# Returned rows two partitions apart, one halved expert fewer, and reordered transfers in a kernel of three expert layers and a convolution

## The chip, the cores and the metric

The kernel runs on one core of one Trainium2 chip. The metric is device time in microseconds (us), lower is better. A core has TensorE (PE in the profile, with PEld for its weight loads), VectorE (DVE), ScalarE (ACT), GpSimd (POOL) and SyncE (SP), which here issues all the DMA transfers.

## The reference

x is (2, 8, 256, 256): two batches b, eight channels or experts e, 256 tokens n, 256 features d. All is float32. Four blocks follow each other, each behind a group norm over pairs of channels:

```python
def _gn(v, G=4, eps=1e-05):
    g = v.reshape(B_, G, C_ // G, H_, W_)
    m, s = mean and var of g over (2, 3, 4)
    return ((g - m) / sqrt(s + eps)).reshape(v.shape)

x = x + L0(_gn(x))      # per expert e: gelu(x[b,e] @ w1[e] + b1[e]) @ w2[e] + b2[e], hidden width 1024
x = x + L1(_gn(x))      # 3x3 convolution over (n, d), 8 to 8 channels, edges repeated,
                        # weights sign(w) * mean(|w|), plus a bias per output channel
x = x + L2(_gn(x))      # like L0
x = x + L3(_gn(x))      # like L0, with the exact gelu
```

So a channel pair must be complete, in both tokens and features, before the group norm of the next block can be applied to it.

## The kernel before

**Data.** Features lie on the partitions: XT holds feature d = 128 c + p at partition p, chunk c. Twenty-four experts E0 to E23 are worked one after the other, eight per layer. An expert has eight units t, one per 128 hidden columns. A unit is six matmuls of the first product (`g1`, line 1016, into a G1 bank) and six of the second (`g2`, lines 1034 to 1039, into an ACC bank). Both products split each operand in a high part (float32r) and the rest: Xh and Xl, W1h and W1l, W2h and W2l, Hh and Hl. ACT makes the high parts and the gelu, DVE the rests by subtraction. TensorE runs `g2` two units behind `g1`. A normal expert has both batches side by side, 512 columns. A halved expert runs its eight units for one batch and then for the other, 256 columns each. Halved are E7, E8 and E9; E8 and E9 are also crossed (E8 batch 0, E9 batch 0, E8 batch 1, E9 batch 1).

**Weights.** SP loads each expert's W1 and W2 (1 MB each) into one W1raw and one W2raw. A load waits until the expert before has been split. ACT (`w_hi`) and DVE (`w_lo`) split an expert's eight pieces k = 0 to 7 in the eight units of the expert before.

**Statistics.** A job J sums a channel pair (`sums`, bn_stats, line 653), aggregates, and TensorE averages mean and variance over the partitions (lines 995 and 1001). POOL raises to the power -0.5 (line 493), DVE writes scale and shift (`scale_shift`), normalises (`norm`, line 709), and `x_hi` and `x_lo` (lines 553 and 714) split the result.

**Convolution.** The results of layer 0 are stored to DRAM by `store_x1` and loaded by `load_xc` into XC, whose partition is 8 j + channel: 16 rows of d (14 results) for 8 channels in one block, 19 blocks per batch, the last one shifted to fit. Two blocks are a tile; there are 20 tiles q, ten per batch, the tenth of a batch with one block. For a tile POOL makes CN (line 499, waits for the rest `Cl` of two tiles before), ACT the high part Ch (617), DVE the rest Cl (894), TensorE six matmuls with BAND (1122), ACT scales in PSUM (622), DVE adds to XC (903). Four PSUM banks rotate, CN has two buffers, Ch and Cl three; Ch and Cl lie on the memory of Hh and Hl.

**The way home.** For each block SP issues `give_back` (line 436): 14 rows of 8 channels, 112 partitions of XC, to 14 adjoining partitions of XT, 8 KB in each. A block that crosses d = 128 takes two. That is 40 transfers. E9's weights are loaded ahead of them. DVE sums batch 0 of channels 0 and 1 (job 9) at tile 17 and waits there for all of batch 0's transfers (`x2_in[0]`); the sums of batch 1 (job 10) are in E9's first unit. SP's queue is in order: the store and load of channel 7 for batch 1, then the `give_back` of tiles 0 to 19, then the next weights.

**The start.** TensorE transposes the first x tiles (982), runs filler matmuls (`stay_busy`, 989, two matmuls per count), and E0 begins when Xh, Xl and the four pieces of W1 are split. E1's pieces are split in the units 0 to 7 of E0. Pairs of experts in the middle of a layer are run in loops with register addresses.

Of the kernel before, what the change touches and what calls it, by code (L numbers as in the profile page):

```python
# [72 lines left out]
def units(E):

    return 2 * HT if isinstance(E, int) and E in HALVED else HT

def order(P):

    if isinstance(P, int) and 2 * P in CROSSED:
        return [(ee, b * HT + t) for b in range(B) for ee in range(2) for t in range(HT)]
    return [(ee, t) for ee in range(2) for t in range(units(2 * P + ee if isinstance(P, int) else None))]

def slots(E, layer=None):

    return HT * (E + sum(E > h for h in HALVED)) if isinstance(E, int) else (  # L90
        HT * E + (len(HALVED) * HT if layer else 0))

def slot_of(E, t, layer=None):

    if isinstance(E, int) and E in CROSSED:
        return slots(C) + (t // HT * 2 + E - C) * HT + t % HT
    return slots(E, layer) + t

def norm_of(E, b):

    return 2 * C + 2 * b + E - C if isinstance(E, int) and E in CROSSED else 2 * E + b

def evicts(E, layer=None):

    return DC * (E + sum(E > h for h in HALVED)) if isinstance(E, int) else (
        DC * E + (len(HALVED) * DC if layer else 0))

def evicts_for(E, b, layer):

    if not isinstance(E, int):
        return evicts(E - 1, layer)
    if E == C - 1:
        return evicts(E) if b else evicts(E - 1)
    if E in CROSSED:
        return evicts(C) + (2 * b + E - C - 1) * DC if b or E > C else evicts(C)  # L120
    return evicts(E) - DC if E == C + 2 else evicts(E - 1)

ONE_BATCH = {7: 0, 8: 1, 9: 0, 10: 1}

def batches(J):

    return (ONE_BATCH[J],) if isinstance(J, int) and J in ONE_BATCH else tuple(range(B))

def jobs_weighed(J, late):

    return B * J - sum(J > j for j in ONE_BATCH) if isinstance(J, int) else B * J - (len(ONE_BATCH) if late else 0)

USUAL = dict(sums=0, aggregate=1, mean=3, deviate=3, variance=5, eps=6, scale=7)

def jobs_of(P, ee, f):

    if not isinstance(P, int):
        if f == 0:
            return [(2 * P + ee, USUAL, 2 * P - 2 if ee else 2 * P + 2, P - 1 if ee else NPAIR)]  # L150
        return [] if ee else [(P + 7, USUAL, 2 * (P - NPAIR * f) + 2, NPAIR)]
    E = 2 * P + ee
    if E == 0:
        return [(1, dict(sums=4, aggregate=5, mean=7, deviate=7), 2, NPAIR)]
    if E == 1:
        return [(1, dict(variance=0, eps=0, scale=1), 2, NPAIR)]
    if E == 7:
        return [(6, dict(sums=0, aggregate=1, mean=4, deviate=4, variance=6, eps=7, scale=8), 4, 2),
                (7, dict(sums=10, aggregate=11, mean=12, deviate=12, variance=13, eps=13, scale=14), 6, 3)]
    if E == C:  # L160
        return [(11, dict(mean=9, deviate=9, variance=11, eps=11, scale=12), 2, NPAIR)]
    if E == C + 1:
        return [(10, dict(sums=0, aggregate=0, mean=2, deviate=2, variance=3, eps=4, scale=4), 0, NPAIR),
                (11, dict(sums=5, more_sums=6, aggregate=7), 2, NPAIR)]
    if P >= 5 and ee == 0 and P + 1 < LAYERS * NPAIR:
        return [(P + 7, USUAL, (2 * P + 2) % C, NPAIR)]
    return []

def job_for(P, f):  # L170

    if isinstance(P, int):
        return {0: 0, 1: 1, 2: 2, 3: 4, 4: 10}.get(P, P + 6)
    return P if f == 0 else P + 6

def known(value):

    return value if isinstance(value, int) else -1

def norms_of(P, ee, f):

    E = 2 * P + ee
    if isinstance(P, int) and E in HALVED:
        return {C - 1: {}, C: {5: (C + 1, 0, 9), 10: (C + 1, 1, 10), 13: (C + 2, 0, 11)},
                C + 1: {5: (C, 1, 10), 9: (C + 2, 1, 11)}}[E]
    if isinstance(P, int) and E == LAYERS * C - 1:
        return {}
    if ee and f == 0 and not isinstance(P, int):  # L190
        J = 2 * P
    else:
        J = job_for(P + 1 if ee else P, f)
    return {2: (E + 1, 0, J), 4: (E + 1, 1, J)}
# [968 lines left out]
```

## Time and profile before

| | |
|---|---|
| median of 3 runs | 615.67 us (614.67 to 615.85) |
| the profiled execution's own time | 614.43 us |
| its span, first to last instruction | 612.4 us |
| PE busy | 594.5 us (97%) |
| DVE busy | 423.2 us (69%) |
| ACT busy | 430.3 us (70%) |
| POOL busy | 31.3 us (5%) |
| mean granted TensorE clock | 0.989 of full |

Times in the trace are counted from the first instruction. The end of a matmul is modelled, so the distance between two starts says more than one duration. "Idle before" names what ended the wait.

### The profile page before, as it was taken

Reading aid. Unit: us, or ns where it says so; the run is one execution under the profiler, and the core shown is the slowest. Engines: PE = TensorE matmul, PEld = TensorE weight load, DVE = VectorE, ACT = ScalarE, POOL = GpSimd, SP = SyncE. Lnnn points to the kernel's source line nnn. Section 1 sums busy time; section 2 is a strip of 40 time slices with the busy share of each in tenths; the row PEclk is TensorE's granted clock in tenths of the full one; section 3 lists DMA queues with packets and bytes.
Section 4 is the critical chain, followed back from the end, with each engine's and each line's share of the span. In section 5 each row is a group of like instructions: output and inputs, shape, how many; then the busy total and the mean of one; then the engine's idle time right before and its main releaser. Section 6 shows DMA issues by size and latency. Waiting matters only on the chain.

```text
span 612.4 us, 9520 instructions
## 1 busy us (share of the span) xinstructions
PE 594.5 (97%) x2973; PEld 501.0 (82%) x2973; DVE 423.2 (69%) x857; ACT 430.3 (70%) x741; POOL 31.3 (5%) x52
## 2 busy tenths in 40 slices
PE   7999999999999896999999999999999999999997
PEld 7778888888889775999888888888888888888885
DVE  4867968768787796767865866866775675675532
ACT  5766767677777685769867777777767777777743
POOL 2000000000000451000000000000000000000000
PEclk9999999999999997999999999999999999999999
DMA  8673355455363599801332323223234244234001
GB/s 273 188 238 105 113 163 176 119 165 152 108 178 103 197 116 110 177 2 63 109 105 77 130 68 118 88 74 133 70 109 132 86 123 136 86 116 142 17 19 69
DMA packets 56342, 72.80 MB, mean 119 GB/s; under 512 B 4064, under 2 KB 50160, under 8 KB 56304
## 3 DMA queue, kind: packets, MB, share of 16 engines
q1 hardware_dynamic: 56304, 72.33, 41.5%
q8 instruction: 19, 0.31, 0.2%
q14 instruction: 19, 0.16, 0.1%
HBM read 59.70 MB, written 8.42 MB: 111 GB/s over the span
## 4 chain that ended last, share of the span: by engine, by line
PE 87%; DVE 4%; DMA 2%; issue 2%; SPq 2%; POOL 1%; ACT 1%; DVEq 0%; POOLq 0%; ACTq 0%
PE G L1016 42%; PE ACC L1039 14%; PE ACC L1034 14%; PE ACC L1035 14%; DMA W2raw<-in_L_conv_w 1%; DVE Cl L894 1%; DMA XT<-XC 1%; PE TR L1052 1%; SPq L374 1%; DVE XC L903 1%; DVE BN L653 1%; SPq L436 1%; PE ACC L1122 1%; PE TR L982 1%; PE STAT L995 0%
## 5 line engine op out<-in xcount | busy, mean ns | idle before, releaser
L720 DVE TENSOR_TENSOR Hl<-HR,Hh 128x512 fp32r<-128x512 f32 (+1 forms) x216 | 136.2, 631 | 158.8 <-ACT Hh L563 157.5
L559 ACT ACTIVATE HR<-G,BT 128x512 f32<-128x512 f32 (+1 forms) x216 | 138.3, 640 | 137.1 <-PE G L1016 135.9
L1016 PE MATMUL G<-Xh,W1l 128*128 128x512 f32 (+1 forms) x432 | 163.9, 379 | 3.3 <-issue 1.9
L1016 PE MATMUL G<-Xl,W1h 128*128 128x512 f32 (+1 forms) x432 | 158.7, 367 | 0.0
L1016 PE MATMUL G<-Xh,W1h 128*128 128x512 f32 (+1 forms) x432 | 158.5, 367 | 0.0
L1034 PE MATMUL ACC<-Hh,W2l 128*128 128x512 f32 (+1 forms) x432 | 156.5, 367 | 0.0
L1035 PE MATMUL ACC<-Hh,W2h 128*128 128x512 f32 (+1 forms) x432 | 156.2, 366 | 0.0
L563 ACT ACTIVATE Hh<-HR 128x512 fp32r<-128x512 f32 (+1 forms) x216 | 126.3, 585 | 8.7
L1039 PE MATMUL ACC<-Hl,W2h 128*128 128x512 f32 (+1 forms) x432 | 123.5, 367 | 0.6 <-DVE Hl L720 0.6
L1016 PEld LDWEIGHTS G<-Xh,W1l 128*128 128x128 f32 x432 | 82.0, 190 | 16.1 <-issue 2.2
L1016 PEld LDWEIGHTS G<-Xh,W1h 128*128 128x128 f32 x432 | 81.9, 189 | 13.6
L1034 PEld LDWEIGHTS ACC<-Hh,W2l 128*128 128x128 f32 x432 | 81.8, 189 | 13.4
L1035 PEld LDWEIGHTS ACC<-Hh,W2h 128*128 128x128 f32 x432 | 81.8, 189 | 13.2
L1016 PEld LDWEIGHTS G<-Xl,W1h 128*128 128x128 f32 x432 | 82.1, 190 | 11.5
L1039 PEld LDWEIGHTS ACC<-Hl,W2h 128*128 128x128 f32 x432 | 78.2, 189 | 14.5 <-DVE Hl L720 1.3
L699 DVE TENSOR_TENSOR W2l<-W2raw,W2h 128x512 fp32r<-128x512 f32 x96 | 65.6, 686 | 4.2 <-ACT W2h L546 3.6
L699 DVE TENSOR_TENSOR W1l<-W1raw,W1h 128x512 fp32r<-128x512 f32 x96 | 65.5, 686 | 2.7 <-ACT W1h L546 2.5
L546 ACT ACTIVATE W2h<-W2raw 128x512 fp32r<-128x512 f32 x96 | 58.9, 616 | 3.6 <-DMA W2raw<-in_L_conv_w 3.6
L546 ACT ACTIVATE W1h<-W1raw 128x512 fp32r<-128x512 f32 x96 | 58.6, 617 | 2.1 <-DMA W1raw<-in_L_conv_w 2.1
L653 DVE BATCH_NORM_STATS2 BN<-XT 128x6 f32<-128x512 f32 (+1 forms) x60 | 37.3, 680 | 3.2 <-DMA XT<-XC 3.2
L493 POOL TENSOR_TENSOR RS<-VE,half 128x2 f32<-128x2 f32 (+1 forms) x18 | 12.8, 708 | 489.4 <-DVE VE L677 489.4
L714 DVE TENSOR_TENSOR Xl<-XN,Xh 128x512 fp32r<-128x512 f32 x48 | 32.9, 686 | 0.6 <-ACT Xh L553 0.4
(73 smaller groups left out, 357.4 us busy)
## 6 DMA issues: line engine op xcount, KB each, us to landing
W1raw<-in_L_conv_w SPq DMA_DIRECT2D x24, 1024.0 KB, 5.1
W2raw<-in_L_conv_w SPq DMA_DIRECT2D x24, 1024.0 KB, 5.6
x_scratch<-XT SPq DMA_DIRECT2D x16, 256.0 KB
out_x<-OUTT SPq DMA_DIRECT2D x16, 256.0 KB, 2.2
XC<-x_scratch SPq DMA_DIRECT2D x16, 252.0 KB
XT<-XC SPq DMA_DIRECT2D x34, 112.0 KB
NAT<-in_x SPq DMA_DIRECT2D x6, 512.0 KB, 8.4
NAT<-in_x SPq DMA_DIRECT2D x4, 256.0 KB, 3.6
```

Source lines behind the costliest of these rows:

```text
L493: nc.gpsimd.tensor_tensor(RS[:, bs], VE[:, bs], half[:, bs], ALU.pow).then_inc(rs_done, 1)
L546: nc.scalar.activation(dst, src, ACT.Copy).then_inc(whi, 1)
L559: nc.scalar.activation(HR[:, t % 2, 0:n], G1[t % 2][:, 0:n], func, bias=BT[:, bass.ds(col, 1)]).then_inc(gelu_done, 1)
L563: nc.scalar.activation(Hh[:, t % RING, 0:n], HR[:, t % 2, 0:n], ACT.Copy).then_inc(hhi, 1)
L653: nc.vector.bn_stats(BN[:, b, i], at).then_inc(bn_done, 1)
L699: nc.vector.tensor_tensor(dst, src, high.bitcast(F32), ALU.subtract).then_inc(wlo, 1)
L714: nc.vector.tensor_tensor(Xl[:, par, :, b], XN[:, b], Xh[:, par, :, b].bitcast(F32), ALU.subtract).then_inc(xlo, 1)
L720: nc.vector.tensor_tensor(Hl[:, t % RING, 0:n], HR[:, t % 2, 0:n], Hh[:, t % RING, 0:n].bitcast(F32), ALU.subtract).then_inc(hlo, 1)
L1016: ins = nc.tensor.matmul(G1[t % 2][:, 0:width(b)], w[:, ee, c, col], rhs, start=n == 0, stop=n == len(parts) - 1)
L1034: nc.tensor.matmul(banks[m][:, 0:n], W2l[:, ee, t8, col], high, start=t8 == 0, stop=False)
L1035: nc.tensor.matmul(banks[m][:, 0:n], W2h[:, ee, t8, col], high, start=False, stop=False)
L1039: ins = nc.tensor.matmul(banks[m][:, 0:n], W2h[:, ee, t8, col], Hl[:, t % RING, 0:n], start=False, stop=t8 == HT - 1)
```

## The change

- **XT's order of features, from the convolution on.** Feature d = 128 c + 64 g + i lies at partition 2 i + g. `give_back` writes 14 rows to partitions two apart. A block is cut at every 64 features, so there are 44 transfers. W1 of the layers 2 and 3 is loaded by two transfers, each to every second partition. W2's columns are put in that order by `w_hi` and `w_lo`, which write every second element. The last evacuation (`out_evac_step`) reads PSUM with a step of two elements. The bias columns are laid out by two transposes more, behind a copy on POOL.
- **Halved experts.** Only E7 and E8 are halved, not crossed; E9 runs at 512 columns. The passes are PA and PB (E7, batch 0 and 1), PC and PD (E8), then one per expert.
- **SP's queue.** E9's weights are loaded behind all the `give_back`. `load_xc` is one transfer per batch in place of four.
- **Convolution.** The edges of XC are doubled by POOL. CN has four buffers and waits for the matmuls of four tiles before, not for Cl. Ch and Cl have memory of their own. ACT doesn't scale: DVE multiplies and adds from PSUM in one instruction, and the convolution's bias is folded into the next statistics and b2. Three PSUM banks rotate. The first tile is issued ahead of E7's last `g2`. Job 9's sums, and their wait, stand at tile 13; job 10's in unit 3 of PC.
- **The start.** W1 of E0 comes in two halves. The add of epsilon stands ahead of the first `w_lo`; only two pieces of W1 are needed for the first unit. The fillers are 12 + 4 + 4 + 3 behind the variance in place of 16. E1's pieces 0 to 7 are split in the units 3, 4, 4, 5, 6, 6, 7, 7 of E0.
- **All loops** over pairs are written out.

```diff
-HALVED = (C - 1, C, C + 1)
-CROSSED = (C, C + 1)
-CRING = 3
+GROUPS = 2
+SPAN = PART // GROUPS
+CRING, HRING = 4, 3
+BANKS = 3
+HALVED = (C - 1, C)
+LAST = dict(evict=0, sums=1, aggregate=1, mean=3, eps=5, scale=6)
+FIRST = dict(sums=13, aggregate=13, mean=14, eps=15, scale=16, split=17)
...
+        if E == 1:
+            steps = [3, 4, 4, 5, 6, 6, 7, 7]
+        elif E == C:
+            steps = [unit(q, t) for q in (PA, PB) for t in (1, 3, 5, 7)]
+        elif E == C + 1:
+            steps = [unit(PC, 5), unit(PC, 7)] + [unit(PD, t) for t in (1, 2, 3, 5, 6, 7)]
...
+    (0, (1,), 0.5, dict(sums=unit(PC, 3), aggregate=unit(PC, 3), mean=unit(PC, 4), variance=unit(PC, 5),
+                        eps=unit(PC, 6), scale=unit(PC, 6))),
...
+                    sp.dma_start(XC[e:PART:C, b, :, 1:N + 1], windows).then_inc(done, 16)
...
+            def give_back(q):
+                b, own = blocks(q)
+                sp.wait_ge(cadded, q + 1)
+                for k in range(own.start, own.stop):
+                    for j, n, c, g, i in rows_back(k):
+                        sp.dma_start(XT[GROUPS * i + g:GROUPS * (i + n):GROUPS, c, :, b],
+                                     XC[j * C:(j + n) * C, b, k, 1:N + 1]).then_inc(x2_in[b], 16)
...
-                if b == 0:
-                    load_w1(1, 1, C + 1)
-                    load_w2(1, 1, C + 1)
...
+            for q in range(B * TILES):
+                give_back(q)
+            load_w1(C + 1)
+            load_w2(C + 1)
...
             def normalise_tile(q):
-                wait(pool, clo, q - 1)
+                wait(pool, conv_mm, q - CRING + 1)
...
+            def w2_stored(w, E):
+                if E < C:
+                    return w2_columns(w, E)
+                return w.rearrange("p t (c i g) -> p (t c) g i", c=DC, g=GROUPS)
...
+            def conv_add(q):
+                dve.wait_ge(conv_mm, q + 1)
+                nc.vector.scalar_tensor_tensor(at, conv_bank(q)[:, 0:w * N].rearrange("p (k n) -> p k n", k=w),
+                                               conv_mean[:, 0:1], at, ALU.mult, ALU.add).then_inc(cadded, 1)
...
+                if u == unit(PC, 0):
+                    conv_low(0)
+                    for q in range(B * TILES):
+                        if q + 1 < B * TILES:
+                            conv_low(q + 1)
+                        conv_add(q)
+                        beside_tile(q)
...
             variance_over_partitions(0)
+            stay_busy(12)
...
-            stay_busy(16)
+            for b in range(B):
+                stay_busy(4)
+                pe.wait_ge(xn_done, b + 1)
+            stay_busy(3)
+            for u in range(UNITS):
+                if u == unit(PC, 0):
+                    g2(u - 2)
+                    conv_tile(0)
+                    g2(u - 1)
+                    for q in range(1, B * TILES):
+                        conv_tile(q)
+                        if q == FIRST["mean"]:
+                            mean_over_partitions(FIRST_JOB)
```

## Rows read from the trace of the kernel before

**Rows 1.** Chain that ended last, two units in layer 2: start, us, what

```profile
355.63 1.36 PE G L1016 x6
358.35 1.36 PE G L1016 x6
```

**Rows 2.** Timeline of PE, convolution to E10: start, us, instructions, idle before

```profile
204.40 0.94 PE L1122 MATMUL ACC<-Ch,BAND 128*128 128x512 f32 x3 [1.30 <-ACT Ch L617]
...
235.68 0.58 PE L995 MATMUL STAT<-MV,ones_mean 128*128 128x1 f32 x2 [3.72 <-DVE MV L660]
...
238.84 0.42 PE L1001 MATMUL STAT<-Q,ones_mean 128*128 128x1 f32 x2
...
242.79 0.36 PE L1016 MATMUL G<-Xh,W1l 128*128 128x256 f32 x1 [1.95 <-issue]
...
248.87 0.28 PE L1016 MATMUL G<-Xh,W1l 128*128 128x256 f32 x1
...
250.31 0.28 PE L1016 MATMUL G<-Xh,W1l 128*128 128x256 f32 x1
...
294.61 0.40 PE L1016 MATMUL G<-Xh,W1l 128*128 128x512 f32 x1
```

**Rows 3.** Windows of PE: stretch, length, PE busy (count), clock, DMA share, GB/s

```profile
234.00:235.00 1.00, 0.00 (x0) 0.54 0.93 68
...
240.00:241.00 1.00, 0.85 (x4) 0.54 1.07 99
...
245.00:246.00 1.00, 1.00 (x7) 0.50 1.03 130
```

**Rows 4.** Timelines of DVE and POOL, 220 to 235

```profile
220.15 0.89 DVE L894 TENSOR_TENSOR Cl<-CN,Ch 128x516 fp32r<-128x516 f32 x1
...
221.57 0.89 DVE L894 TENSOR_TENSOR Cl<-CN,Ch 128x516 fp32r<-128x516 f32 x1
...
234.10 1.29 DVE L653 BATCH_NORM_STATS2 BN<-XT 128x6 f32<-128x512 f32 x2 [3.16 <-DMA XT<-XC]
...
221.14 0.77 POOL L499 TENSOR_SCALAR CN<-XC,CST 128x516 f32<-128x516 f32 x1 [0.64 <-DVE Cl L894]
```

**Rows 5.** SP's queue: timeline, and line 436 by tile (ns min/median/max)

```profile
206.47 0.37 SPq L390 DMA_DIRECT2D x_scratch<-XT  x1
...
208.80 0.88 SPq L405 DMA_DIRECT2D XC<-x_scratch  x1
...
L436 SPq DMA_DIRECT2D XT<-XC x40: 675/801/890, 211.6 to 245.0; - x40
```

**Rows 6.** DMA, 227 to 229 (packets, MB, share), and an issue's landing

```profile
q1 hardware_dynamic: 252, 0.23, 101.0%
...
out_x<-OUTT SPq DMA_DIRECT2D x16, 256.0 KB, 2.2
```

**Rows 7.** Timelines of PE and ACT, 9 to 40: start, us, instructions, idle before

```profile
9.48 0.38 PE L1001 MATMUL STAT<-Q,ones_mean 128*128 128x2 f32 x2
...
11.46 3.78 PE L989 MATMUL G<-ones_mean,ident 128*128 128x128 f32 x32
16.42 0.50 PE L1016 MATMUL G<-Xh,W1l 128*128 128x512 f32 x1 [1.18 <-DVE Xl L714]
...
34.98 0.50 PE L1016 MATMUL G<-Xh,W1l 128*128 128x512 f32 x1
...
38.19 0.74 PE L1039 MATMUL ACC<-Hl,W2h 128*128 128x512 f32 x2 [0.64 <-DVE Hl L720]
...
39.23 0.48 PE L1016 MATMUL G<-Xh,W1l 128*128 128x512 f32 x1
...
33.20 0.63 ACT L546 ACTIVATE W2h<-W2raw 128x512 fp32r<-128x512 f32 x1 [3.63 <-DMA W2raw<-in_L_conv_w]
```

**Rows 8.** Groups by shape, DVE: busy us, mean ns

```profile
L780 DVE TENSOR_TENSOR band_tap<-conv_sign,mask 128x128 f32<-128x128 f32 x9 | 3.0, 388 | 0.0
...
L785 DVE TENSOR_TENSOR band_sum<-band_tap 128x128 f32<-128x128 f32 x3 | 0.9, 294 | 0.1
```

More of the change, by code:

```diff
@@ L38 @@
 LAYERS = 3
+EXPERTS = LAYERS * C
 BCOLS = C * HT + C * DC
@@ L46, with pass_of, first_pass, last_pass @@
 NBLK = -(-D // OUTR)
-LASTROW = D + 2 - ROWS
+DP = OUTR * (NBLK - 1) + ROWS
 NP = N + 2
-DP = D + 2
 TILES = -(-NBLK // 2)
-CRING = 3
+CRING, HRING = 4, 3
+BANKS = 3
+BOTH = tuple(range(B))
+HALVED = (C - 1, C)
+PASSES = [(E, bs) for E in range(EXPERTS) for bs in (((0,), (1,)) if E in HALVED else (BOTH,))]
+UNITS = HT * len(PASSES)
+def pass_of(E, b):
+    return next(p for p, (e, bs) in enumerate(PASSES) if e == E and b in bs)
+def first_pass(E):
+    return pass_of(E, 0)
+def last_pass(E):
+    return pass_of(E, B - 1)
@@ new lines, in unit, with halved, width, split_no @@
+def unit(p, t):
+    return HT * p + t
+def halved(p):
+    return len(PASSES[p][1]) == 1
+def width(p):
+    return N * len(PASSES[p][1])
+SPLITS = [(p, b) for p, (E, bs) in enumerate(PASSES) for b in bs]
+def split_no(p, b):
+    return SPLITS.index((p, b))
+def evicted_by(p):
+    return DC * (p + 1)
+PA, PB, PC, PD = (pass_of(E, b) for E in HALVED for b in range(B))
+def split_steps():
+    at = {}
+    for p, b in SPLITS[2:]:
+        if p == PD:
+            at[unit(PC, 7)] = (p, b)
+        elif p != PC:
+            at[unit(p - 1, 2 + 2 * b)] = (p, b)
+    return at
@@ new lines, with weight_steps @@
+AHEAD = 5
+def weight_steps():
+    at = {k - AHEAD: [(0, k)] for k in range(AHEAD, 8)}
+    for E in range(1, EXPERTS):
+        p = first_pass(E) - 1
+        steps = [unit(p, t) for t in range(HT)]
+        if E == 1:
[4 more added lines that the diff above has]
+            steps = [unit(PC, 5), unit(PC, 7)] + [unit(PD, t) for t in (1, 2, 3, 5, 6, 7)]
+        for k, u in enumerate(steps):
+            at.setdefault(u, []).append((E, k))
+    return at
@@ new lines, with jobs_at, job_of @@
+NJOBS = len(JOBS)
+CONV_JOBS = {b: [J for J, (e, bs, of, _) in enumerate(JOBS) if of == 0 and b in bs] for b in range(B)}
+LAST_CONV_JOB = {b: max(CONV_JOBS[b]) for b in range(B)}
+LAST_JOB = LAST_CONV_JOB[B - 1]
+FIRST_JOB = LAST_JOB + 1
+def jobs_at(stage, u):
+    return [J for J, job in enumerate(JOBS) if job[3].get(stage) == u]
+def job_of(E, b):
+    f, e = divmod(E, C)
+    of = (-1, 0.5, 1)[f]
+    return next(J for J, job in enumerate(JOBS) if job[2] == of and job[0] == e - e % 2 and b in job[1])
@@ L54, in rows_back, with weighed @@
+def weighed(J):
+    return sum(len(job[1]) for job in JOBS[:J])
 def rows_back(k):
     d, end = OUTR * k, min(OUTR * (k + 1), D)
-    j = d - LASTROW + 1 if k == NBLK - 1 else 1
+    j = 1
     parts = []
     while d < end:
-        c = d // PART
-        n = min(end, (c + 1) * PART) - d
-        parts.append((j, n, c, d % PART))
+        n = min(end, (d // SPAN + 1) * SPAN) - d
+        parts.append((j, n, d // PART, d % PART // SPAN, d % SPAN))
         d, j = d + n, j + n
     return parts
-def pieces_back():
-    return sum(len(rows_back(k)) for k in range(NBLK))
@@ L72 @@
-HALVED = (C - 1, C, C + 1)
-CROSSED = (C, C + 1)
[L76 to L91, printed above, removed]
@@ L94, in slot_of @@
[L94 to L121, printed above, removed]
@@ L126 @@
[L126 to L167, printed above, removed]
@@ L170, in job_for @@
[L170 to L194, printed above, removed]
@@ L197, in split_at, with blocks, tile_width @@
-def split_at(P, ee, t):
-    E = 2 * P + ee
-    if isinstance(P, int):
-        if E == LAYERS * C - 1:
-            return None
-        if E == C:
-            return t + 4 if t < 4 else None
-        if E == C + 1:
-            return t - HT if t >= HT else None
-    return t if t < HT else None
+PIECES_BACK = sum(len(rows_back(k)) for k in range(NBLK))
+def blocks(q):
+    b, i = divmod(q, TILES)
+    return b, slice(2 * i, min(2 * i + 2, NBLK))
+def tile_width(q):
+    b, own = blocks(q)
+    return own.stop - own.start
@@ L1140 @@
+            for u in (UNITS - 2, UNITS - 1):
+                g2(u)
+            for b in range(B):
+                out_transpose(EXPERTS - 1, b, (TR, G1[0])[b])
 _INS = {"x": (B, C, N, D)}
```

958 lines of the change are left out of this document (466 added, 492 removed).

## The prediction

> **What bounds the kernel now.** I read the page first: PE busy 97% of the span at a mean clock of 0.989, the other engines 70% or less. Then the chain that ended last. In the expert layers it is PE alone: units of 12 matmuls follow each other every 2.72 us [rows 1], so 227 ns a matmul of 512 columns. A halved unit takes 1.44 us for half the columns (from 248.87 to 250.31 [rows 2]); both batches together cost 2.88, 0.16 more than 2.72, so a halved expert costs 1.3 us more. The change adds nothing to PE's work there. What it can move is where PE waits: the start, and the stretch from the convolution to E10.
>
> PE's timeline shows that stretch [rows 2]. The first convolution matmul is at 204.40 behind 1.30 idle. Before 235.68 there are 3.72 idle: TensorE's mean of job 9 waits for sums, which DVE starts at 234.10 behind 3.16 us of waiting for the transfers home [rows 4]. Then comes the clock: by 234 to 235 it is at its lower level, 1.2 GHz, where it stays until 240 to 241 [rows 3]. From 235.68 to 238.84 PE does a mean and one tile [rows 2], some 2.7 us for the tile where the pace had been 1.42 (from 220.15 to 221.57 [rows 4]). E8 starts at 242.79 behind 1.95 idle, and the clock falls once more (245 to 246: 0.50 [rows 3]). E8's fifth `g1` is at 248.87 [rows 2]; at full pace three units of 1.44 after 242.79 would be 247.11. That fall cost 1.76.
>
> So what sets this stretch is when `x2_in` is complete. SP issues from 211.6 to 245.0, 40 transfers of 675 to 890 ns, median 801 [rows 5]; with the gap between two, 0.85 us each. The DMA engines meanwhile show 101% busy at 0.23 MB in 2 us, 115 GB/s [rows 6]. A transfer of 112 KB then needs 1.0 us, a little more than its issue, and the landing falls behind: batch 0's 20 are issued by 228.6 and land at 234.1.
>
> **Start.** TensorE's variance matmul is at 9.48. The fillers after it were 16 counts in 3.78 us, 0.236 each [rows 7]. There will be 23, 5.4 us, and about 0.4 us for five small transposes: from 9.9 to 15.7. Behind this cover lies the chain of E0's input. It ended at 16.4 before, and DVE now has two W1 subtractions less in front of Xl, instructions like Cl, which is 0.7 to 0.9 [rows 4]: 15.0 at the latest, and less as epsilon no longer waits for W1. So PE's own fillers decide, and E0 starts at 15.7 instead of 16.42 [rows 7]: -0.7. If the fillers are shorter than I make them, the chain of E0's input takes their place. The second piece: ACT waited 3.63 us for W2raw until 33.20, and E0's last unit took 34.98 to 39.23, 4.25 us where 2.72 and 0.25 for a mean are due [rows 7]. E1's W2 pieces now come in unit 6, where ACT arrives at about 34, behind the landing. That gives 1.3. Start: -2.0.
>
> **The way home.** Times here are on the clock of the trace before, without the 2.0. POOL doubles the edges and makes CN ahead of E7's end, and Ch has its own memory, so the first tile runs at about 202.5 instead of 204.4, and E7's last evacuation ends at 205.7 instead of 206.5. Store and load of channel 7 lie between this and the first `give_back`: 206.47 to 208.80 to 211.6 before [rows 5]. The load is now one transfer instead of four, about 0.7 us: first `give_back` at 208.9. It is queued behind the store and the load, and E9's weights are queued behind it.
>
> Cost of one issue: not in the trace for this shape, since the destination gets one dimension more. Bounds from the nearest rows: 0.675, the smallest of line 436, and 0.88, the load of line 405 (14 partitions and three dimensions) [rows 5]; with the gap of 0.04 that is 0.72 to 0.92. A bound below for all of it would be 0.66, if also the gap went. I take 0.85 for the mean, as before: the dimension more makes it dearer, seven short pieces of 22 make it cheaper. Batch 0: 22 x 0.85 = 18.7, plus 2.2 to land (as the 256 KB of out_x [rows 6]), is 229.8 against 234.1.
>
> What the spread is worth: 115 GB/s was the drain [rows 6]. If it stays, 2.1 MB take 18.3 us, as long as the issue, and the lag of some 3 us stays in part, up to +1.0 us. If it doubles, issue alone decides. 
>
> **Convolution.** DVE has Cl and the add per tile. Before, Cl took 0.89 where POOL's CN of 0.77 ran into it, and the tiles came every 1.42 [rows 4]. I keep 1.4 per tile, and 2.1 us for job 8's small work: 205.7 + 13 x 1.35 - 0.6 for the half tile + 2.1 = 224.8 when DVE comes to tile 13 and stops for `x2_in[0]`. Queued behind that wait are the tiles 14 to 19 on DVE, and so PE, whose mean stands behind tile 14: PE stops at 226.4. From 229.8 on: two sums at 0.65 [rows 4], bias and aggregate, 1.85, and PE resumes at 231.7 after 5.3 us. By the rows of before that is enough for the lower clock, for some 5 us after resuming [rows 3]. Then DVE's rest: 5.5 tiles at 1.2 (6.6), deviation, epsilon, scale, one norm and Xl 2.0, and 2.6 of waiting for PE at 1.2 GHz. Sum 13.1: E8 at 242.9, as good as before.
>
> **E8 and E9.** From E8's start to E10's third unit before: 242.79 to 294.61, 51.8 [rows 2]. Now: two `g1` alone 1.44, 14 halved units 20.2, two mixed units of 2.08 and six of 2.72 for E9 20.5, two of E10 5.4, four averages 0.9: 48.4. Of the 3.4 saved, 1.76 is the second fall of the clock, which I leave out as E8 now follows without a long gap, and 1.3 E9. But job 10's sums in PC's unit 3 wait for all 44 transfers: 208.9 + 44 x 0.85 + 2.2 = 248.5, plus 1.9 for sums and aggregate, 250.4. PE asks for the mean 5.8 after E8's start, at 248.7. It stops 1.7. So E10's third unit is at 250.4 + (48.4 - 5.8) = 293.0 against 294.61: -1.6. E9's W1, queued behind the 44, is issued at 246.5 and lands 5 us on, at about 251.5, when ACT comes to its first piece (252): covered, worth 1 to 2 us if the issue is slower.
>
> **Small things.** W2's steps of two elements on DVE and ACT: the nearest row is a read with a step of nine, 388 ns against 294 for 128 elements [rows 8], so at most 0.4 us per piece, four per expert, hidden in DVE's 30% idle; two evacuations at the very end could show it, 0 to +0.8; I take 0. Written-out loops: 0, as PE had no gap at a loop's end. Layers 2 and 3 otherwise keep their 2.72.
>
> **Sum.** -2.0 - 1.6 = -3.6. On the profiled 614.4 us (span 612.4) that is 610.8. The profiled run is 1.2 us under the median of 615.67, so the median becomes 612.0. A measurement of this kernel can tell about 0.2%, 1.2 us.
>
> **Rivals.**
> (a) The return is early. If an issue costs 0.66 to 0.72, batch 0 is home at 225.6 to 227, DVE hardly waits at tile 13 and the clock stays up: E8 at 235.7 to 237, no stop in PC. E10's third unit 8.5 to 10 earlier: 602.5 to 605. For it: DVE's wait is the largest term and everything hangs on one price. Against it: the median is 801 ns, and a shape with a dimension more has no reason in the trace to be cheaper.
> (b) SP's queue is the brake, slower. E10's third unit comes at 208.9 + 44 c + 2.2 + 1.9 + 42.6 = 255.6 + 44 c for an issue of c: at 0.93 the gain of the start is used up, at 0.97 it is +1.7, and the late E9 weights and a clock fall in PC's stop add up to 3. 617 to 620. Against it: 0.92 is the dearest row.
> (c) POOL blocks DVE. CN no longer waits for Cl, so each Cl may meet a whole CN: +0.6 a tile. DVE comes to tile 13 at 233, the wait is gone, but the six last tiles are slow too: E8 at 247, E10 +2: 615 to 616, no change. The Trainium skill (SBUF — State Buffer, Who interferes with whom) has GpSimd and a VectorE instruction with two SBUF inputs exclude each other for a whole instruction; the 0.89 agrees.
> (d) The start gives nothing, because the chain of E0 ends behind the fillers: 614.
>
> **Chances.** Forecast with its own range of 609.5 to 614: 0.46. (a) 0.24. (b) 0.14. (c) and (d) 0.16. Faster by over 0.2% 0.69, within 0.15, slower 0.16. The range reaches from (a) to the near end of (b): 603 to 617.5.
>
> **What would show it.** E0's first `g1` near 15.7, no ACT wait at W2. Line 436: 44 issues, near 0.81, first at about 207 (208.9 less 2.0); DMA share below 100%. DVE's wait at bn_stats of tile 13, about 5 us, PE's idle and the lower clock behind it; a second stop before the mean in PC. Wrong if the issues cost less than 0.75, if Cl's mean goes over 1 us, or if the clock falls in E8 again.

## The result, and the profile after

The changed kernel takes 619.23 us (median of 4, 618.62 to 620.21), the kernel before 615.17 in the same runs: ratio 1.0076, 95% interval 1.006 to 1.0092. It is slower by 0.8%; 612.0 was forecast, and 619.23 lies above the range of 603 to 617.5. The profiled execution took 618.62 us with a span of 616.8.

First TensorE's timeline (start, us, instructions, idle before), for [rows 2]:

```profile
203.84 0.93 PE L1047 MATMUL ACC<-Ch,BAND 128*128 128x512 f32 x3 [0.90 <-ACT Ch L616]
...
233.05 0.59 PE L984 MATMUL STAT<-MV,ones_mean 128*128 128x1 f32 x2 [4.84 <-DVE MV L699]
...
241.34 0.97 PE L1047 MATMUL ACC<-Ch,BAND 128*128 128x512 f32 x3 [1.45 <-ACT Ch L616]
...
244.12 0.28 PE L1011 MATMUL G<-Xh,W1l 128*128 128x256 f32 x1
...
251.35 0.38 PE L984 MATMUL STAT<-MV,ones_mean 128*128 128x1 f32 x2 [1.22 <-DVE MV L699]
...
258.80 0.35 PE L1011 MATMUL G<-Xh,W1l 128*128 128x256 f32 x1 [2.42 <-issue]
...
267.24 0.51 PE L1033 MATMUL ACC<-Hl,W2h 128*128 128x256 f32 x2 [0.26 <-DVE Hl L758]
269.90 0.38 PE L990 MATMUL STAT<-Q,ones_mean 128*128 128x2 f32 x2 [0.62 <-DVE Q L709]
...
299.07 0.39 PE L1011 MATMUL G<-Xh,W1l 128*128 128x512 f32 x1
```

The first tile is 0.56 earlier than before, E8 starts 1.3 later (244.12 against 242.79), and E10's third unit is 4.5 later (299.07 against 294.61 [rows 2]). So most of the loss lies behind E8's start, where before PE had no wait at all from 255 to 305. The 4.5 carries to the end: the last expert's chain ends 4.4 later (601.19 to 605.62).

SP's queue, and DVE at tile 13, for [rows 4, 5]:

```profile
211.07 36.41 SPq L460 DMA_DIRECT2D XT<-XC  x44
...
231.00 1.29 DVE L684 BATCH_NORM_STATS2 BN<-XT 128x6 f32<-128x512 f32 x2 [3.32 <-DMA XT<-XC]
...
247.53 1.39 SPq L398 DMA_DIRECT2D W1raw<-in_L_conv_w  x2
```

The 44 issues cost 0.83 each (36.41/44, waits for the adds included) where I had 0.85; they begin at 211.07, not at 206.9. Windows (stretch, length, busy us of PE, PEld, DVE, ACT and POOL, clock, DMA share, GB/s), for [rows 3, 6]:

```profile
225.00:227.00 2.00, 2.00 (x10) 1.53 (x9) 2.00 (x4) 0.88 (x3) 1.28 (x3) 1.00 0.30 78
230.00:235.00 5.00, 1.95 (x6) 1.66 (x7) 3.83 (x11) 0.00 (x0) 0.00 (x0) 0.54 0.40 112
235.00:240.00 5.00, 4.88 (x18) 3.66 (x16) 3.11 (x10) 0.00 (x0) 1.49 (x2) 0.77 0.39 107
240.00:245.00 5.00, 3.40 (x20) 2.81 (x21) 3.54 (x7) 1.46 (x3) 0.00 (x0) 1.00 0.41 113
245.00:250.00 5.00, 5.00 (x42) 4.88 (x41) 2.31 (x6) 3.86 (x10) 0.00 (x0) 1.00 0.55 112
```

The DMA engines are at 30 to 55% where they had 101% [rows 6]: the backlog is gone. The clock goes to 1.2 GHz once in this execution, around the 4.84 us of idle PE, and not again in E8. Last the chain that ended last (start, us, what), from the end of E7 to E9:

```profile
202.24 2.78 POOL CN L542 x2
205.71 0.70 DVE Cl L826
207.07 0.78 DVE XT L772 x2
...
227.84 0.81 SPq L460
228.69 2.29 DMA XT<-XC
231.00 1.30 DVE BN L684 x2
233.63 2.79 PE ACC L1047 x6
...
246.82 0.67 SPq L460
247.53 0.69 SPq L398
248.26 6.19 DMA W1raw<-in_L_conv_w
261.55 2.40 DVE BN L684 x4
```

It names four places: POOL's first two CN, batch 0's landing, E9's W1 behind the row of issues, and DVE's sums in PD. The experiments take them up. "W1" in the chain turned out to be the least of them.

### The profile page after: what moved, and what is told of

Its sections match the earlier page's. It is cut to its first block, busy times and chain, and to the rows that moved or that the text cites. A ratio compares the mean times of both kernels' runs of the same rounds, so it can differ in the third digit from the quotient of the medians.

```text
span 616.8 us, 8582 instructions
## 1 busy us (share of the span) xinstructions
PE 593.6 (96%) x2893; PEld 496.5 (80%) x2893; DVE 427.5 (69%) x898; ACT 417.2 (68%) x706; POOL 36.1 (6%) x57
## 4 chain that ended last, share of the span: by engine, by line
PE 86%; DVE 5%; SPq 3%; DMA 3%; ACT 1%; issue 1%; POOL 1%; DVEq 0%; ACTq 0%
PE G L1011 41%; PE ACC L1028 13%; PE ACC L1033 13%; PE ACC L1029 13%; SPq L460 2%; DMA NAT<-in_x 2%; PE ACC L1047 1%; DVE XC L834 1%; DMA W1raw<-in_L_conv_w 1%; PE TR L1060 1%; DVE Cl L826 1%; DVE BN L684 1%; PE TR L971 1%; POOL CN L542 0%; PE TR L1047 0%
## 5 line engine op out<-in xcount | busy, mean ns | idle before, releaser
L1011 PE MATMUL G<-Xh,W1l 128*128 128x512 f32 (+1 forms) x416 | 160.2, 385 | 2.4 <-issue 2.4
L1011 PE MATMUL G<-Xh,W1h 128*128 128x512 f32 (+1 forms) x416 | 155.1, 373 | 0.0
L1011 PE MATMUL G<-Xl,W1h 128*128 128x512 f32 (+1 forms) x416 | 151.3, 374 | 0.1
L1011 PEld LDWEIGHTS G<-Xh,W1l 128*128 128x128 f32 x416 | 78.4, 188 | 14.9 <-issue 2.6
L1028 PEld LDWEIGHTS ACC<-Hh,W2l 128*128 128x128 f32 x416 | 78.3, 188 | 14.1
L1011 PEld LDWEIGHTS G<-Xh,W1h 128*128 128x128 f32 x416 | 78.3, 188 | 14.0
L1029 PEld LDWEIGHTS ACC<-Hh,W2h 128*128 128x128 f32 x416 | 78.3, 188 | 13.9
L1011 PEld LDWEIGHTS G<-Xl,W1h 128*128 128x128 f32 x416 | 78.2, 189 | 12.5 <-DVE Xl L752 0.3
L595 ACT ACTIVATE Xh<-XN 128x512 fp32r<-128x512 f32 x48 | 29.6, 618 | 18.7 <-DVE XN L746 18.7
L684 DVE BATCH_NORM_STATS2 BN<-XT 128x6 f32<-128x512 f32 x60 | 37.4, 680 | 3.4 <-DMA XT<-XC 3.3
```

Of the source, the lines that this page charges most:

```text
L595: nc.scalar.activation(Xh[:, par, :, b], XN[:, :, b], ACT.Copy).then_inc(xhi, 1)
L684: nc.vector.bn_stats(BN[:, J % 2, b, i], XT[:, :, e + i, b]).then_inc(bn_done, 1)
L1011: ins = nc.tensor.matmul(G1[u % 2][:, 0:n], w[:, par, c, col], rhs, start=i == 0, stop=i == len(parts) - 1)
L1028: nc.tensor.matmul(acc(p, m), W2l[:, par, t, col], high, start=t == 0, stop=False)
L1029: nc.tensor.matmul(acc(p, m), W2h[:, par, t, col], high, start=False, stop=False)
```

## Experiments

The kernel before was run beside all of them on the same chip; ratios are to it. Its median was 614.53 beside experiments 1 to 4, 614.60 beside 5 to 8 (on another chip), 616.08 beside 9 to 11 and 614.65 beside 12 to 14, so times of different groups are best compared by their ratios. "E8" and "third" are the starts of E8's first `g1` and of E10's third unit in the profiled run.

**1. E9's weights ahead of the way home.**

```diff
                load_xc(C - 1, (b,), x1_last[b], 48, xc_last[b])
+                if b == 0:
+                    load_w1(C + 1)
+                    load_w2(C + 1)
...
-            load_w1(C + 1)
-            load_w2(C + 1)
```

> Edit: E9's W1 and W2 are issued as in the kernel before, in front of the give_back transfers; when they are split stays as it is. Theory A (SP's 44 issues hold back all that is queued behind them, E9's weights among it): in the changed kernel ACT stops 0.95 us for W1raw and DVE's epsilon of job 10 stands behind that split until 256.30, so PD's first g1 is at 258.80 where about 257 is due (E8 at 244.1, eight halved units of 1.44, the 1.22 stop for the mean). Without it: W1 home long before PC, PD's first g1 near 257, the rest of PD as full as before: 617 to 618 where the changed kernel has 619.2. Rival B (PD itself is too full on DVE, and its start doesn't matter): 619. Rival C (two transfers of 1 MB in front of channel 7's store delay the first give_back by up to 1 us): 619 to 620.

618.31 us, ratio 1.0051 (1.0035 to 1.0068); the interval overlaps with the change's, so the gain of 0.9 us by the medians is uncertain. Its timeline of PE:

```profile
252.27 0.38 PE L985 MATMUL STAT<-MV,ones_mean 128*128 128x1 f32 x2 [1.22 <-DVE MV L700]
258.97 0.36 PE L1012 MATMUL G<-Xh,W1l 128*128 128x256 f32 x1 [1.68 <-issue]
```

The wait for W1raw is gone and PD's first `g1` is not earlier (E8 had begun 0.9 later, at 245.03, so PC is 0.74 shorter). Behind the DMA in the chain lay a second one of almost the same length: DVE's epsilon of job 10 stands in PC's unit 6, behind Hl, and from there to the end of Xh it takes 2.4 us. Behind this stop of 1.68 us the clock fell a second time, inside E8, which it doesn't do in the change's execution behind 2.42 us. First a window of experiment 1, then one of the change:

```profile
260.00:264.00 4.00, 4.00 (x22) 4.00 (x22) 2.69 (x5) 1.94 (x5) 0.00 (x0) 0.57 0.00 0
```
```profile
256.00:262.00 6.00, 3.45 (x28) 3.08 (x27) 3.79 (x12) 3.15 (x7) 0.54 (x1) 1.00 0.01 3
```

PD took 14.3 us in both, so this fall cost next to nothing: DVE sets PD's pace.

**2. Job 9's sums at tile 15.**

```diff
-FIRST = dict(sums=13, aggregate=13, mean=14, eps=15, scale=16, split=17)
+FIRST = dict(sums=15, aggregate=15, mean=16, eps=17, scale=18, split=19)
```

> Edit: the sums of job 9 move from tile 13 to tile 15, the steps behind them by two as well. Theory A (the last of 44 transfers decides): the stop of 3.3 us on DVE at tile 13 and the lower clock behind it go, E8 starts at 238 to 239 instead of 244.1, but batch 1 is home only at 249, so PE stops some 6 us in PC before the mean of job 10, the clock falls there instead, and PD starts within 1 us of 258.8: 618.5 to 620.5. Rival (the stop at tile 13 is the loss, and E8's start carries on to the end): 5 us faster, 614.

619.99 us, ratio 1.0077 (1.0058 to 1.0096): no gain, as theory A has it. PE's timeline shows that most of the stop moved:

```profile
240.03 0.36 PE L1011 MATMUL G<-Xh,W1l 128*128 128x256 f32 x1 [1.68 <-issue]
251.13 0.59 PE L984 MATMUL STAT<-MV,ones_mean 128*128 128x1 f32 x2 [4.78 <-DVE MV L699]
260.36 0.36 PE L1011 MATMUL G<-Xh,W1l 128*128 128x256 f32 x1 [1.38 <-issue]
```

E8 is 4.1 earlier, PE then stands 4.78 us for batch 1, and the clock is at 1.2 GHz through the next units of PC:

```profile
251.00:257.00 6.00, 5.87 (x27) 5.88 (x28) 1.92 (x7) 2.15 (x5) 0.00 (x0) 0.50 0.73 260
```

In one point theory A doesn't hold: PE still stops 1.99 us before job 9's mean, and the clock is at 0.50 from 234 to 237, so E8 starts at 240.03 and not at 238 to 239.

**3. Rows in adjacent partitions.** `-GROUPS = 2`, `+GROUPS = 1`.

> Edit: GROUPS = 1, so rows lie in adjacent partitions again: 40 transfers home, E9's W1 in one transfer, no strided W2 pieces; all else as changed. Theory A (issues, with the landing lag a smaller term): four issues less end the row 3.3 us earlier, but the DMA engines go back to about 100% at 115 GB/s, so 2.1 MB land 3 to 5 us behind their issue instead of 2.3: batch 1 home at 249 to 251, time within 1.2 us of 619.2. Rival B (the spread layout is the loss, by its four more issues and its strided pieces): 616 to 617. Rival C (the spread gains as much as its port share suggests): 621 to 623.

619.48 us, ratio 1.0084 (1.0066 to 1.0102): the same as the change. An issue costs the same (median 807 ns; first the change, then experiment 3, ns min/median/max):

```profile
L460 SPq DMA_DIRECT2D XT<-XC x44: 669/807/912, 211.1 to 246.8; - x44
```
```profile
L460 SPq DMA_DIRECT2D XT<-XC x40: 677/807/912, 210.3 to 246.7; - x40
```

What differs is the landing. Batch 0's row of the chain, and a window of batch 1's transfers with the share of the DMA engines:

```profile
226.46 4.32 DMA XT<-XC
```
```profile
235.00:237.00 2.00, 2.00 (x7) 1.61 (x7) 0.76 (x4) 0.00 (x0) 0.57 (x1) 0.50 0.97 124
```

The last of batch 0's issues ends 2.2 earlier (226.46 against 228.69) and its data take 4.32 instead of 2.29 to land, so batch 0 is home at 230.8 as against 231.0. The two cancel: with SP as only issuer the spread rows, their four more issues and W2's strided pieces together bring nothing and cost nothing that can be measured. The rest of the forty end late because the last tiles' adds are late, behind the stop, not because an issue is dearer.

**4. ACT issues nine of the 44.**

```diff
+        ON_ACT = (1, 3, 5, 7, 9, 11, 13, 15, 17)
...
                         conv_high(q)
+                        if q - 3 in ON_ACT:
+                            send(act, q - 3, True)
```

(`send` issues the last transfer of such a tile on ACT, all others on SP.)

> Edit: ACT issues one transfer home for each odd tile up to 17 (9 of the 44), three tiles behind. Theory A (SP's row of issues sets E8, job 10 and E9's weights): SP has 35 issues, 211.1 to 240.1; batch 0 home at about 227.5 where DVE comes to tile 13 at 226.9, so next to no stop and no lower clock, E8 at about 238, batch 1 home at 242.5, E9's W1 home near 247; PD and E9 as full as before: E10's third unit at 289 to 292 instead of 299.2, 609 to 612. Rival B (DVE's work per tile and in PD sets the time, whoever issues): E8 early, but 2 us are all that arrives: 617. Rival C (ACT has 0.64 us of Ch in a tile of 1.42 and an issue costs 0.83, so tiles with one take 1.5 to 1.6 and Ch comes late): 613 to 615.

613.05 us, ratio 0.9976 (0.9963 to 0.9988). A fifth of the issues moved, and 1% of the time goes. The time lies 1 us above theory A's 609 to 612. DVE's wait at tile 13, and the window behind it:

```profile
227.78 1.29 DVE L696 BATCH_NORM_STATS2 BN<-XT 128x6 f32<-128x512 f32 x2 [0.85 <-DMA XT<-XC]
```
```profile
230.00:232.00 2.00, 2.00 (x8) 1.64 (x9) 1.95 (x6) 0.00 (x0) 0.00 (x0) 0.73 0.31 88
```

0.85 us instead of 3.32. DVE came to tile 13 at 226.93, as theory A had it, so ACT's issues did not slow the tiles (rival C). PE was idle for 2.38, since the sums and the aggregate come on top, and the clock still went down (0.73 here, 0.50 from 231 to 234). E8 starts at 240.55 and not at 238 as theory A had it.

**5. Both: ACT's share and tile 15.**

> Edit: ACT issues nine of the 44 transfers, and the sums of job 9 move to tile 15 (both edits, each tried alone before: 613.05 and 619.99). Theory A (whoever is late with batch 1 sets the end; SP's row was the reason the later sums alone gave nothing): with SP relieved the stop of 2.38 us on PE and the lower clock from 230 to 235 go, E8 starts 3 to 4 us earlier than 239.9, batch 1 is home near 242 as job 10 asks for it, and the time comes out at 609 to 610.5. Rival (batch 1's return still sets PD): 612.5 to 613.5, with a stop in PC that is longer by what E8 gained.

611.68 us, ratio 0.9958 (0.994 to 0.9977); E8 at 237.33, PE's stop before the mean 1.35, no fall of the clock. The time lies between theory A's 609 to 610.5 and the rival's 612.5 to 613.5. The later sums, worth nothing alone, now bring about 1.4 us by the medians; the intervals overlap, so the size is uncertain. The 1.22 before job 10's mean and 1.71 before PD stay, though batch 1 is no longer late.

**6. E8 and E9 crossed again.** (E9's weights early and split in PC, job 10's steps in E9's batch 0.)

```diff
-PASSES = [(E, bs) for E in range(EXPERTS) for bs in (((0,), (1,)) if E in HALVED else (BOTH,))]
+CROSSED = [(C - 1, (0,)), (C - 1, (1,)), (C, (0,)), (C + 1, (0,)), (C, (1,)), (C + 1, (1,))]
+PASSES = [(E, BOTH) for E in range(C - 1)] + CROSSED + [(E, BOTH) for E in range(C + 2, EXPERTS)]
```

> Edit: E8 and E9 are halved and crossed again, as in the kernel before (E8 batch 0, E9 batch 0, E8 batch 1, E9 batch 1), with E9's weights issued ahead of give_back and split in PC; all else as changed. The early weights alone gave 618.31. Theory A' (job 10's steps, from sums in PC's unit 3 to Xh in its last, need some 9.5 us by DVE's program order, while three and a half halved units give 6: 1.22 us stop at the mean, 1.7 to 2.4 at PD's first g1, some 2.3 in PD, whoever issues the transfers): these 5 to 6 us go, E9 costs 1.3 more in halves: 613.5 to 615. Rival (what comes after the return is shifted with it, whatever the order): 618 to 620.

615.79 us, ratio 1.0025 (1.0014 to 1.0037), 0.8 above the 613.5 to 615 of theory A'. It holds at less than its size. E8 at 243.68, third at 295.86: 52.2 us against 55.0 in the change. One stop is left, 0.86 before the second half of E8.

**7. Crossed, with ACT's share and tile 15.**

> Edit: crossed order, ACT's share of the issues and the sums of job 9 at tile 15 together. Theory A + A' (two separate losses): the gains add: E8 at 236, then as the kernel before without a stop up to E10: 604 to 607. Rival (both edits cure the same wait, batch 1's): no better than the better of the two alone, 609 or more.

609.89 us, ratio 0.993 (0.9909 to 0.9951). Below either alone by the medians, though its interval still touches experiment 5's (0.994 to 0.9977): that points to two losses, and experiment 11 bears it out. It is 2.9 above the most that I had expected, with a profiled run that began E0 2.7 us later than the change's (18.88 against 16.18).

**8. Only DVE's order in PC and PD.**

```diff
-                        eps=unit(PC, 6), scale=unit(PC, 6))),
+                        eps=unit(PC, 5), scale=unit(PC, 5))),
...
-            at[unit(PC, 7)] = (p, b)
+            at[unit(PC, 6)] = (p, b)
...
-            steps = [unit(PC, 5), unit(PC, 7)] + [unit(PD, t) for t in (1, 2, 3, 5, 6, 7)]
+            steps = [unit(PC, t) for t in (0, 1, 2, 4, 7)] + [unit(PD, t) for t in (1, 3, 5)]
```

> Edit: E9's weights issued ahead of give_back; job 10's epsilon and scale in PC's unit 5 instead of 6, PD's norm in 5 and Xl in 6; E9's splits in PC 0, 1, 2, 4, 7 and PD 1, 3, 5. Nothing of SP's row or the order of passes is changed. Theory A' (DVE's program order in PC and PD is the loss behind E8): PD's first g1 comes 1.3 to 1.7 us earlier than 258.97 and the stops in PD stay away: 616 to 617 where the early weights alone had 618.31. Rival (only the landing of batch 1 matters): 618.3.

617.19 us, ratio 1.0054 (1.0034 to 1.0073). By the ratio it can't be told from experiment 1; by the trace the stop before PD is gone, PE waits 2.23 before the mean instead of 1.22, and the third unit is at 297.72 (299.27 in experiment 1). PD's first `g1` came 0.9 earlier, at 258.07, where 1.3 to 1.7 was expected. That 1.5 us I count as read from one execution each, not as timed, all the more as the clock fell in PD in experiment 1 and not here.

**9. Adjacent rows with ACT's share.** Experiment 4 with GROUPS = 1.

> Edit: ACT issues nine transfers (as in the run that had 613.05), and GROUPS = 1 on top, so rows lie in adjacent partitions. With adjacent rows alone SP's 40 issues took 37.14 us, 0.93 each, while the DMA engines were 82 to 97% busy at 124 to 135 GB/s. Theory P (adjacent rows are held by the DMA engines, so the spread is worth nothing while SP issues alone and worth all of ACT's help once the issues are shared): 40 transfers of 115 KB at about 125 GB/s need 36.7 us from 210.3 on, batch 0 is home at 229 to 231, E8 as late as with SP alone: 617 to 620. Rival (the issue alone decides, and 0.93 was the issue's own price): 612.5 to 614.

621.53 us, ratio 1.008 (1.005 to 1.0111), where the spread rows have 0.9976. Theory P had 617 to 620: four executions are there, at 617.9 to 618.7 and a mean clock of 0.991 to 0.994, the profiled one (618.66) among them. The other five took 621.5 to 623.8, at 0.987 to 0.992; none of those has a trace. The direction is theory P's, but "0.93 each" in its text was misread: 37.14/40 holds waits for adds, and the issues' median is 807 ns in all of these kernels. The drain shows in the landing instead. The chains' rows for batch 0, experiment 4 and then experiment 9:

```profile
224.74 3.01 DMA XT<-XC
```
```profile
222.74 7.77 DMA XT<-XC
```

and a window of experiment 9:

```profile
225.00:227.00 2.00, 1.96 (x9) 1.24 (x7) 1.44 (x3) 0.74 (x2) 0.95 (x2) 1.00 1.02 110
```

ACT's help ends the issues of batch 0 3.7 us earlier than in experiment 3, and the landing takes nearly all of it back (4.32 to 7.77): home at 230.5. The engines are at 102% for 110 GB/s. So the spread is worth 1.0% here by the ratios, 0.7% by the two profiled executions (618.66 and 614.31), and nothing in experiment 3.
**10. E8's splits back in PA.**

```diff
-            steps = [unit(q, t) for q in (PA, PB) for t in (1, 3, 5, 7)]
+            steps = [unit(PA, t) for t in range(HT)]
```

> Edit: E8's eight splits stand in PA's units 0 to 7 (as in the kernel before) instead of half in PA and half in PB. In the changed kernel DVE's split at 203.23, the bn_stats at 202.31 and Cl stand beside POOL's second CN, which ends only at about 205.0, and the evacuation of PB is at 206.98 where I had predicted its end at 205.7 less 2.0. Theory D (these splits push the first tiles and so the first give_back): first give_back 0.7 to 1.5 us earlier than 211.07, all of it carried to the end: 617.8 to 618.5. Rival (POOL's CN waits for other work of DVE just as long): 619.2.

616.47 us beside 616.08, ratio 1.0004 (0.9984 to 1.0025): the largest single undoing of the change, more than theory D had. E7's first `g1`, and DVE, POOL and ACT at its end, first of the change:

```profile
175.31 0.28 PE L1011 MATMUL G<-Xh,W1l 128*128 128x256 f32 x1
...
200.04 0.15 DVE L715 TENSOR_SCALAR VE<-STAT 128x1 f32<-128x1 f32 x1
...
202.24 6.87 POOL L542 TENSOR_SCALAR CN<-XC,CST 128x516 f32<-128x516 f32 x6 [1.05 <-issue]
...
203.23 0.69 DVE L739 TENSOR_TENSOR W2l<-W2raw,W2h 128x512 fp32r<-128x512 f32 x1
...
205.04 1.39 ACT L616 ACTIVATE Ch<-CN 128x516 fp32r<-128x516 f32 x2 [1.34 <-POOL CN L542]
...
206.98 0.87 DVE L772 SCALAR_TENSOR_TENSOR XT<-ACC,BT,XT 128x256 f32<-128x256 f32 x2
```

and of experiment 10:

```profile
174.94 0.28 PE L1011 MATMUL G<-Xh,W1l 128*128 128x256 f32 x1
...
198.63 0.15 DVE L715 TENSOR_SCALAR VE<-STAT 128x1 f32<-128x1 f32 x1
...
200.88 4.87 POOL L542 TENSOR_SCALAR CN<-XC,CST 128x516 f32<-128x516 f32 x5 [0.66 <-POOL XC L534]
...
202.64 0.64 ACT L616 ACTIVATE Ch<-CN 128x516 fp32r<-128x516 f32 x1 [0.29 <-POOL CN L542]
...
204.92 0.88 DVE L772 SCALAR_TENSOR_TENSOR XT<-ACC,BT,XT 128x256 f32<-128x256 f32 x2
```

Two things go. Epsilon of E7's job no longer stands behind a split of 0.69 (VE 1.4 earlier, and so POOL's first CN). And POOL's second CN, which dragged on to 205.0 beside DVE's split, bn_stats and Cl, is done at 202.6: Ch(1) is 2.4 earlier. The evacuation comes 2.06 earlier, the first `give_back` at 209.02 instead of 211.07, E8 at 241.79, third at 296.31. Of these differences 0.37 is no gain of the edit: E7 began that much earlier in this execution (174.94 against 175.31). Counted from there the first `give_back` comes 1.7 earlier. From the first tile to the evacuation it is 3.13 us or more in all kernels with splits in PB and 2.43 to 2.45 in the five without. The Trainium skill (SBUF — State Buffer, Who interferes with whom) has GpSimd instructions that read SBUF and VectorE instructions with two SBUF inputs exclude each other; the first two CN, 2.78 us together in the change's chain and 1.74 in experiment 10's, agree. The shares of the two causes were not separated.

**11. The best of all.** Experiment 6, E8's splits in PA, x pair 1 ahead of W2, tile 13, and ACT issues one transfer of the tiles 1, 2, 4, 5, 7, 8 and 9, of batch 0 alone.

> Edit: crossed order of E8 and E9 with the early weights; ACT issues seven transfers of batch 0 only (tiles 1, 2, 4, 5, 7, 8, 9); sums of job 9 at tile 13; x pair 1 ahead of W2 at the start; E8's splits in PA. Theory A + A' : batch 0 has 15 issues on SP, over at 223, home at 225.5, ahead of DVE's tile 13 at 226.9, so PE has no stop and the clock stays up; E8 starts at 236.5 to 237.5; batch 1, home at 244, is asked for at 251 only: 606 to 608.5, below the 609.89 of the crossed kernel with ACT's share. Rival (ACT's issues of 0.83 beside Ch of 0.64 slow the tiles of batch 0 above 1.42, or the start's spread hides it): 609 to 611.

607.94 us beside 616.08: ratio 0.9866 (0.9839 to 0.9893), clearly below both kernels and in the expected 606 to 608.5. Its rows of DVE and PE:

```profile
224.71 1.27 DVE L698 BATCH_NORM_STATS2 BN<-XT 128x6 f32<-128x512 f32 x2
```
```profile
226.73 0.38 PE L998 MATMUL STAT<-MV,ones_mean 128*128 128x1 f32 x2 [1.43 <-DVE MV L713]
233.13 0.97 PE L1061 MATMUL ACC<-Ch,BAND 128*128 128x512 f32 x3 [1.46 <-ACT Ch L625]
```

DVE doesn't wait for the transfers at all, the clock stays at 1.00 from 225 on, E8 is at 235.92 and the third unit at 288.12.

**12. The same with job 9's later steps at tiles 15, 17, 18, 19.**

> Edit: the kernel that had 607.94, with job 9's mean, epsilon, scale and split at tiles 15, 17, 18 and 19 instead of 14, 15, 16 and 17. In that kernel PE stopped 1.43 us for the mean and 1.46 for Ch of tile 18, which stands behind Xh in ACT's queue. Theory (only the program order of ACT and DVE makes these two stops): both go, but the chain from epsilon to Xh (2.4 us) then stands behind tile 17, so a stop of 0.5 to 1.5 is left before E8: 606.5 to 607.5. Rival (DVE is full in these tiles, the stops only move): 608.

608.68 us, ratio 0.9915 (0.9885 to 0.9946), beside a kernel before of 614.65: not better, as the rival had it (608). The two stops became 1.31 (Cl) and 1.67 (before E8).

**13. Two rearrangements undone.** Crossed order, and E8's splits in PA; all else of the change stays.

> Edit: E8 and E9 crossed with the early weights, and E8's splits in PA: two of the change's rearrangements are undone, while the start, the spread rows with 44 transfers, POOL's edges and CN and the written-out loops stay. Alone the two gave 1.0025 and 1.0004 of the kernel before where the change has 1.0076. Theory (two separate losses, each of 0.5 to 0.7%): they add, ratio 0.994 to 0.998 to the kernel before, which is then what the rest of the change is worth. Rival (both shorten the same chain): ratio 1.000 or more.

614.27 us, ratio 0.9992 (0.9977 to 1.0007). E8 at 241.58, third at 293.75 (before: 294.61). The two losses seem to add only in part: 0.84% of the 1.23% that they were worth alone, a gap of little more than the intervals allow. With both undone the change is worth nothing that can be measured, not the 0.2 to 0.6% that I expected.

**14. The best with adjacent rows.** Experiment 11 with GROUPS = 1.

> Edit: the kernel that had 607.94 with GROUPS = 1 (rows in adjacent partitions, 40 transfers, 7 of them issued by ACT). Theory P (adjacent rows are held by the DMA engines at 110 to 125 GB/s, whoever issues): batch 0 home at 227 to 229 instead of before 224.7, a stop of 3 to 4 us at tile 13, the clock falls, 3 to 6 us slower than 607.94: ratio 0.992 to 0.997 to the kernel before where that one had 0.9866. Rival (the spread costs as much in issues as it gives): 0.9866.

612.58 us, ratio 0.996 (0.994 to 0.9981) against 0.9866 with spread rows; experiment 12, run beside it with spread rows, had 0.9915. Batch 0's last issue ends at 220.97 and lands 7.03 later; DVE waits 1.41 at tile 13 (3 to 4 was expected), PE 2.95, and from 230 to 235 the clock is at 0.66.

## Why the prediction was wrong, by its steps

**Right.** The price of an issue (0.83, I had 0.85). The backlog of the DMA engines goes. DVE waits for batch 0 at tile 13: 3.32 us, I had about 5 between 224.8 and 229.8. E8 follows 13.1 us after batch 0's landing: 231.00 and 244.12, the sum was 13.1. In part that is luck: its terms have no stop for Ch, and that took 1.45. The clock doesn't fall again in E8 in the profiled execution; experiments 1 and 2 show that it can. The stop before job 10's mean: 1.22, I had 1.7.

**"First `give_back` at 208.9"**, 206.9 less the start, was 211.07, and this is the step that failed first. It carried batch 0's landing (231.00 against 227.8) and E8 (244.12 against 240.9) with it: +3.2. Of the 4.2 (211.07 less 206.9), 1.3 is the start. The rest lies ahead of the store: E7's last evacuation ended at 207.85, where the prediction's 205.7, less the start, gives 203.7; from there to the first `give_back` it is 3.2 in both. Some 1.7 is an edit that I put at nothing, E8's splits moved into PB: DVE there has the job's epsilon and the first Cl, POOL the first CN. Experiment 10 gives back this 1.7, and experiment 13 gets to 208.17. Another 1.1 is the first tile itself. I had it at 202.5, 26.5 behind E7's first `g1` (176.02), because POOL makes CN ahead of E7's end; it is 27.55 behind even in experiment 10 (202.49 less 174.94) and was 28.38 in the kernel before. CN needs the scale of E7's statistics: in the change it starts at 202.24, behind DVE's VE (200.04) and ST. So of the 1.9 that I gave this term 0.8 was there in experiment 10, and nothing in the change (28.53). DVE reached tile 13 at 227.68 (231.00 less 3.32) and not at 222.8: the 4.2, and 0.7 because the sum took 1.35 a tile where its text keeps 1.4.

**"Now ... : 48.4", plus 1.7.** From E8 to E10's third unit it was 55.0 instead of 50.1. The count of PE's work was right, the waits in it weren't: I followed job 10 to its mean and not on to PD's Xh. From the mean on lie variance, epsilon in unit 6, RS, scale, norm and Xh, and that gave another stop of 2.42 at PD's first `g1`. PD itself took 14.3 (258.80 to 273.1) where 12.0 was due: I put its splits, four bn_stats (2.40 in the chain) and norms down as covered. These two make 4.7 of the 4.9. In the crossed order this way is 52.2 (experiments 6, 11 and 13), and 54.2 with only the early weights. So E9's 1.3 us for being halved bought eight halved units of slack for job 10, worth more than it cost.

**"Start: -2.0"** was -0.7 at the last unit of E6 (172.59 against 173.30). E0 began at 16.18 (15.58 in experiment 2, 15.7 forecast), and TensorE waited 1.08 for x pair 1:

```profile
18.90 0.66 PE L971 MATMUL ACC<-ident,NAT 128*128 128x128 f32 x4 [1.08 <-DMA NAT<-in_x]
```

The variance matmul stood at 10.17 where I had kept the 9.48 of before. W1 in two transfers and the biases, one issue of which took 1.09, put the load of x pair 1 1.1 later on SP's queue (8.56 against 7.45). Its landing varies: over the runs the wait was 0 to 1.26.

**The rivals.** Rival (b) had the sign and the time (617 to 620), but not the cause: the issue cost less than its 0.93. Its late weights of E9 are real, but worth 0.9 us at most by the medians (experiment 1). (c), POOL and DVE in each other's way, was real in E7's last units and not in the tiles (Cl's mean 0.73). (a) was what experiments 5 and 11 made, DVE's wait for batch 0 gone and the clock up, and they came to 611.68 and 607.94, not to its 602.5 to 605. (d) holds in part: the start gave 0.7 of its 2.0.

**Shown:** SP as only issuer holds batch 0's return (4, 11), the DMA engines hold it once rows are adjacent and ACT helps (9, 14); E8's splits in PB cost more than 0.3% (10); E9's uncrossing with its weights and splits behind the return costs about 0.5% (6). **Open:** how the cost in experiment 10 divides between DVE's order and POOL's exclusion; whether experiments 10 and 6 fall short of adding in 13, and why; what x pair 1's place at the start is worth by itself, as it ran only within 11, 12 and 14.

## What to carry to other kernels

When one queue issues a row of small transfers, read the issue and the drain apart: read the drain by the time from the last issue to the landing; a faster drain (here the spread rows) was worth nothing here until a second engine shared the issues, and then some 0.5 to 1%. When a pass is shortened or reordered, follow each chain through it to the next pass's first operand, by the queue of every engine in program order, and cost the steps that were moved to make room too: the two edits that I took as covered were most of the loss. And when the chain names a DMA, ask what would be next: here taking it away gave 0.9 us at most of the 6.19 it showed.
